# Linear attention inside a four-layer kernel: two batches' exponents moved to the head's begin, one score moved ahead of a product, and ten loops written out

## The reference, cut to what matters

```python
# attention B, batch size 4, 256 tokens, 16 heads, key size 128, value size 256
q = silu(causal_group_conv(h @ Wq.T));  k = silu(causal_group_conv(h @ Wk.T))   # 4 taps, one group per head
v = h @ Wv.T
gate = sigmoid(h @ Wg.T + bg);  beta = sigmoid(h @ Wb.T + bb)
def step(St, xs):                       # over the 256 tokens
    St = bt[..., None, None] * St + kt[..., None] * vt[:, :, None, :]
    ot = einsum('bhk,bhkv->bhv', qt, St) * gt[..., None]
out = outs @ Wo.T
```

## Time and profile before

| | |
|---|---|
| median of the runs | 1483.29 us |
| profiled execution | 1482.8 us, span 1481.0 us |
| TensorE busy | 1420.5 us, 96% of the span |
| VectorE, ScalarE, GpSimd busy | 61%, 58%, 55% |
| granted TensorE clock, mean | 0.992 of full |
| attention B, heads | about 752 to 1214 us of the span |
| feed-forward layers | about 452 to 704 us and 1214 to 1481 us |

### The profile page before, as it was taken

The page is one execution under the profiler, slowest core; times in us unless marked ns, Lnnn a source line. Parts: engine busy times, 40 slices in busy tenths (PEclk is TensorE's granted clock), DMA queues, the critical chain, the costliest instruction groups (busy, mean ns, idle before and its releaser), DMA issues. The chain is left out here.

```text
span 1481.0 us, 24095 instructions
## 1 busy us (share of the span) xinstructions
PE 1420.5 (96%) x8354; PEld 1228.3 (83%) x8360; DVE 901.3 (61%) x1719; ACT 861.7 (58%) x1737; POOL 819.8 (55%) x685
## 2 busy tenths in 40 slices
PE   7799999999999999999999999999999989999998
PEld 5589888898876778887689999999999976778886
DVE  6776766767665434334777777777777764443434
ACT  5566656666654433333587777777777755343332
POOL 4744444444433555554367767776777624455553
PEclk9999999999999999999999999999999999999999
DMA  2122232322311111110222212221222011111111
GB/s 82 32 69 72 70 70 69 71 67 71 73 31 50 43 53 43 43 52 21 79 69 71 64 54 60 71 64 54 61 70 64 19 39 33 43 42 53 42 53 39
DMA packets 48603, 82.48 MB, mean 56 GB/s; under 512 B 4256, under 2 KB 29984, under 8 KB 48288
## 3 DMA queue, kind: packets, MB, share of 16 engines
q1 hardware_dynamic: 48544, 81.70, 20.5%
HBM read 80.38 MB, written 1.31 MB: 55 GB/s over the span
## 5 line engine op out<-in xcount | busy, mean ns | idle before, releaser
L424 POOL TENSOR_TENSOR ms_a_lo<-m_a,ms_a_hi 128x384 fp32r<-128x384 f32 x128 | 129.9, 1015 | 200.4 <-ACT ms_a_hi L420 200.4
L1112 DVE TENSOR_TENSOR f_h<-f_sc,ps 128x512 f32<-128x512 f32 x112 | 76.4, 682 | 182.6 <-POOL f_sc L1044 182.6
L243 PE MATMUL ps<-xn_hi,fgu_hi 128*128 128x512 f32 x448 | 177.1, 395 | 5.1 <-DVE f_h L1112 4.8
L245 PE MATMUL ps<-xn_hi,fgu_lo 128*128 128x512 f32 x448 | 178.4, 398 | 0.0
L244 PE MATMUL ps<-xn_lo,fgu_hi 128*128 128x512 f32 x448 | 177.0, 395 | 0.0
L1114 DVE TENSOR_TENSOR fh_lo<-f_h,fh_hi 128x512 fp32r<-128x512 f32 x112 | 107.2, 957 | 98.3 <-ACT fh_hi L420 98.3
L993 ACT ACTIVATE f_s<-ps 128x512 f32<-128x512 f32 x112 | 66.7, 597 | 161.2 <-PE ps L245 161.0
L1044 POOL TENSOR_TENSOR f_sc<-f_s,coef_r 128x512 f32<-128x512 f32 x88 | 114.0, 1296 | 67.5 <-ACT f_s L993 67.5
L420 ACT CAST fh_hi<-f_h 128x512 fp32r<-128x512 f32 x112 | 69.1, 617 | 124.9 <-DVE f_h L1112 124.8
L424 POOL TENSOR_TENSOR fd_lo<-fw_raw,fd_hi 128x256 fp32r<-128x256 f32 x56 | 52.1, 930 | 125.8 <-ACT fd_hi L420 125.8
L243 PE MATMUL ps<-xn_hi,aw_hi 128*128 128x512 f32 x256 | 109.0, 426 | 7.4 <-DVE bmat_lo L727 7.4
(11 more groups left out here) (281 smaller groups left out, 4820.4 us busy)
## 6 DMA issues: line engine op xcount, KB each, us to landing
fw_raw<-ffn_w SPq DMA_DIRECT2D x56, 384.0 KB, 3.0
rows_a<-a_rows_d SPq DMA_DIRECT2D x64, 256.0 KB, 4.8
wconv_raw<-b_conv SPq DMA_DIRECT2D x16, 513.0 KB, 3.6
aw_raw<-a_heads SPq DMA_DIRECT2D x32, 256.0 KB, 5.2
wvo_raw<-b_vo SPq DMA_DIRECT2D x16, 512.0 KB, 3.5
rows_b<-b_rows_d SPq DMA_DIRECT2D x32, 256.0 KB, 4.9
wqk_raw<-b_qk SPq DMA_DIRECT2D x16, 256.0 KB, 4.8
x<-xT SPq DMA_DIRECT2D x2, 512.0 KB, 4.8
```

The lines of the kernel that those rows point to most:

```text
L243: nc.tensor.matmul(o, w[0], v[0], start=first, stop=False, skip_group_check=True)
L245: return nc.tensor.matmul(o, w[1], v[0], start=False, stop=last, skip_group_check=True)
L424: return nc.gpsimd.tensor_tensor(dst[1], src, f32(dst[0]), ALU.subtract).then_inc(sem(done_sem), 1)
L1112: nc.vector.tensor_tensor(f_h[:, c], f_sc[:, c], ps[:, 2 + c, :], ALU.mult).then_inc(sem("f_h"), 1)
```

## The change

In attention B, VectorE makes the exponents of batches 0 and 1 before it turns to the next head's fold and projections, and ScalarE makes their exponentials behind the two casts of k and ahead of the copies of the projections. ScalarE's casts of m_b keep their places among the casts of the values, but for batch 1, which loses the exponential in front. VectorE's exponents get a wait that the two batches of the head before are multiplied. TensorE computes score 2 ahead of value product 0. And all `Fori` loops of attention B and of the feed-forward layers become Python loops, so that their code is written out and the head is a constant.

```diff
@@ b_head_pe
             make("values")
+            b_score_pe(pe, h, p, 2, last)
             b_value_pe(pe, h, p, 0, last)
-            b_score_pe(pe, h, p, 2, last)
             b_score_pe(pe, h, p, 3, last)
@@ b_head_act
             if not last:
                 make("fold")
                 b_k_hi_act(act, h, p)
+                b_score_act(act, h, 0)
+                b_score_act(act, h, 1)
                 make("qk0", "qk1")
+            else:
+                b_score_act(act, h, 0)
+                b_score_act(act, h, 1)
             values = (lambda i: None) if last else (lambda i: b_values_act(act, h + 1, 1 - p, i))
             values(0)
-            b_score_act(act, h, 0)
+            b_split_act(act, h, 0)
             values(1)
-            b_split_act(act, h, 0)
-            b_score_act(act, h, 1)
+            b_split_act(act, h, 1)
             values(2)
-            b_split_act(act, h, 1)
             values(3)
@@ b_exponents_dve
-            if b >= 2:
+            if BATCH * h + b >= 2:
                 dve.wait_ge(sem("b_m_done"), BATCH * h + b - 1)
@@ b_head_dve
-            make("fold", "qk0", "qk1")
             for b in range(2):
                 b_exponents_dve(dve, h, b)
+            make("fold", "qk0", "qk1")
@@ f_pe, f_act, f_pool, f_dve, f_sp, b_pe, b_act, b_dve, b_pool, b_sp: each of the ten loops, as
-            with pe.Fori(0, B_HEADS // 2 - 1) as h2:
+            for h2 in range(0, B_HEADS // 2 - 1):
```

More of the change, by code:

```diff
@@ L919, in f_pe @@
             f_up_pe(pe, f, S_TILES, 0)
-            with pe.Fori(S_TILES // 2, F_TILES // 2 - 1) as i2:
+            for i2 in range(S_TILES // 2, F_TILES // 2 - 1):
                 for p in range(2):
@@ L970, in f_act @@
             f_up_weights_act(act, f, S_TILES + 1, 1)
-            with act.Fori(S_TILES // 2, F_TILES // 2 - 1) as i2:
+            for i2 in range(S_TILES // 2, F_TILES // 2 - 1):
                 for p in range(2):
@@ L1028, in f_pool @@
             pool.wait_ge(sem("f_coef_ready"), f_count(f, "coef_ready", 1))
-            with pool.Fori(S_TILES // 2, F_TILES // 2 - 1) as i2:
+            for i2 in range(S_TILES // 2, F_TILES // 2 - 1):
                 for p in range(2):
@@ L1072, in f_dve @@
                     f_route_dve(dve, f, step)
-            with dve.Fori(S_TILES // 2, F_TILES // 2) as i2:
+            for i2 in range(S_TILES // 2, F_TILES // 2):
                 for p in range(2):
@@ L1121, in f_sp @@
                 sp.dma_start(fw_raw[:, p], ffn_w[p * P:(p + 1) * P, :]).then_inc(sem(f"f_w_loaded{p}"), 16)
-            with sp.Fori(0, F_TILES // 2 - 1) as i2:
+            for i2 in range(0, F_TILES // 2 - 1):
                 for p in range(2):
@@ L1334, in b_act @@
             act.wait_ge(sem("b_ncum"), 1)
-            with act.Fori(0, B_HEADS // 2 - 1) as h2:
+            for h2 in range(0, B_HEADS // 2 - 1):
                 b_head_act(act, 2 * h2, 0, False, True)
@@ L1471, in b_dve @@
             b_make_dve(dve, 0, 0, ["conv1"])
-            with dve.Fori(0, B_HEADS // 2 - 1) as h2:
+            for h2 in range(0, B_HEADS // 2 - 1):
                 b_head_dve(dve, 2 * h2, 0, False)
@@ L1591, in b_pool @@
             b_conv_pool(pool, 0, 0, 1)
-            with pool.Fori(0, B_HEADS // 2 - 1) as h2:
+            for h2 in range(0, B_HEADS // 2 - 1):
                 b_head_pool(pool, 2 * h2, 0, True, True)
@@ L1661, in b_sp @@
                 sp.dma_start(rows_b[:, c], rows_of(b_rows_d, 0, c)).then_inc(sem(f"b_rows_loaded{c}"), 16)
-            with sp.Fori(0, B_HEADS - 2) as h:
+            for h in range(0, B_HEADS - 2):
                 for name, raw, src in B_PARTS:
```

## The result

The changed kernel takes 1490.25 us (median of 5 runs, 1489.03 to 1491.16), the kernel before 1483.29 (five runs by now, 1481.26 to 1484.62): the ratio is 1.0048, 95% interval 1.0033 to 1.0062, so 0.5% slower. The forecast was 1488.9.

What follows compares the result with a forecast made beforehand. TensorE, busy 96% of the span, was taken as the bound, so only its waits or added work matter. Terms -15.0 + 18.8 + 1.8 + 0 = +5.6 us gave 1488.9 us, range 1484.0 to 1494.0.

Steps and rivals of the forecast that it cites:

- The wait that goes: TensorE's wait at value product 0 for GpSimd's low part of the scores vanishes in heads 0 to 14: -15.0 us.
- The wait that comes: TensorE's k projection waits for ScalarE's q copy, delayed by four exponentials: 1.25 us in each of 15 heads, +18.8 us.
- The convolution's third block: TensorE reaches this block too early for VectorE's chain: 0.15 us late, 0.12 more than before, +1.8 us in all.
- The loops: Writing out the loops in attention and feed-forward stages changes nothing: 0, bounds -2 and +2 us.
- the fall of the clock: Rival: the new wait in each head lowers TensorE's clock, 25 us more, 1514 us; chance 0.05.
- The wash: Rival: stalls only change places, exponentials cost 1.1 us a head, convolution's wait does not grow: 1483 to 1486; chance 0.21.
- The faster rival: The q copy has slack, so the exponentials are hidden and only the old wait's removal counts: 1468 us; chance 0.08.

Runs made afterwards that it cites:

- e5: Changed kernel, exponentials of batches 0 and 1 in ScalarE's idle places inside the projections' casts, score 2 back behind value product 0: 1469.62 us, ratio 0.9915.
- e2: Kernel before, loops kept, with only score 2 moved ahead of value product 0: 1483.88 us, ratio 1.0005.
- e4: Changed kernel, exponentials of batches 0 and 1 moved into ScalarE's idle places inside the projections' casts: 1472.48 us, ratio 0.9936.
- e6: Changed kernel, only batch 0's exponentials ahead of the q copy, batch 1's back behind the first values cast: 1480.34 us, ratio 0.9979.
- e7: Changed kernel's order with its loops kept as loops, heads 0 and 1 written out in front: 1494.51 us, ratio 1.0076.
- e3: Changed kernel with score 2 put back behind value product 0: 1487.95 us, ratio 1.0031.
- e1: Kernel before with nothing but its ten loops written out: 1482.16 us, ratio 0.9992.
- e10: The kernel of e5 measured again, loops written out, beside e11 on one chip: 1467.33 us, ratio 0.9893.
- e11: The kernel of e9 measured again, loops kept, beside e10 on one chip: 1467.59 us, ratio 0.9892.
- e9: The order of e5 with loops kept as loops, heads 0 and 1 written out in front: 1467.20 us, ratio 0.9894.
- e8: Changed kernel with the order of e4 in head 0 alone, all other heads as in the changed kernel: 1489.24 us, ratio 1.0044.

## Why the prediction was right

The direction, the place and the sizes of the two large terms held. That the sum in the heads came out to a tenth is partly luck, since small errors of the terms cancel: per head the new wait costs 1.19 net (forecast 1.25), the convolution 0.20 (0.12), and the old wait gives back 1.09 (1.06), which makes 0.30 (0.31). Of the 7.1 us between the spans, by TensorE's landmarks: 0.6 lie ahead of attention B, in code that the change leaves alone (the first load lands 0.9 later); 3.4 in heads 0 and 1, up to head 1's score, of which 1.1 is the clock; 3.6 in the twelve periods up to head 13's, 0.30 each; 0.4 in the next; -0.7 in the last, where the old wait goes and no head is made; -0.2 in the feed-forward layer. Without the clock and the parts outside attention B this is +5.6, the forecast.

1. *The wait that goes.* Right in the whole: it is gone in heads 0 to 14, and e5 shows that with it out, and nothing in its place, the head loses 1.1 us, as counted. Wrong in an aside: "the score alone would have removed two thirds of it". It removes two thirds of the gap, and nothing of the time (e2), for the same chain of VectorE and ScalarE stops TensorE at the convolution. The slack that I had put at 1.2 us is about 1.9: GpSimd's first low part is ready near 918.7, value product 0 starts at 920.67. The text ahead of the prediction says that ScalarE's casts of m_b keep their places, but by the diff each goes one cast of the values earlier (in the trace, 917.11 behind the first and 918.17 behind the second, where they stood behind the second and third). No run takes this apart from the moved exponents, so its share in the gain of 1.1 is not known.
2. *The wait that comes.* Forecast 1.25 us per head; measured 1.12 + 0.11 = 1.23, less the 0.04 of before 1.19, in every head that makes a next one. e4 takes it away by moving two calls, e6 halves it, e7 keeps it without the written-out code: shown.
3. *The convolution's third block.* Forecast 0.12 more than before; measured 0.24 late plus 0.07 restart, 0.2 more than before, and 0.27 by e3. Right kind, half the size. The chain of VectorE took 7.44 us, between the 7.3 and 7.49 that I had worked out, and TensorE's own way 7.20 for 7.22; I had taken 0.15 out of a span of 0.1 to 0.27, counting on 0.15 from the faster answer of written-out code. Against e7 with its loops (7.54) it gave 0.10.
4. *The loops.* Forecast 0; e1 gives -1.0 us with an interval of -2.5 to +0.1, e10 against e11 nothing. In the changed kernel's order the loop form is slower (e7), by 0.1 us a head, at the convolution alone.

The term that was mis-sized is head 0. I had given the fall of the clock a chance of 0.05 as something that strikes all heads or none. It struck only the head where it was already there: the wait of 1.2 us came on top of one of 1.86, and the stretch at 1.2 GHz was longer, 1.1 us. That makes up most of the 1.4 us by which the forecast of +5.6 fell short of the 7.0 of the medians. The long stretch came in three of the four traces with this idle (the changed kernel, its repeat and e3, not e7), so the 1.1 us was no certain part of the change either. My reading that the trace before has one fall of the clock, at the longest idle of the stage, was wrong too: head 15 waits 2.43 us, up to 1199.40, and has a low stretch of its own (0.50 over 1200 to 1203). The Trainium skill, "TensorE: Matmul & The Clock Gate", section HAM oscillation, ties the penalty to idles that are long enough; by that rule, as in the trace, the 0.95 us of the other heads passed at full speed. Length alone does not settle it in these traces, though: 1.86 us lowered the clock in eight kernels of nine, and 2.31 us elsewhere did not.

The wash (0.21) needed the inserted exponentials to cost 1.1 and the convolution nothing; it missed by about 0.1 and 0.2 a head. The bounds of the parts, simply added, give -0.5 to +14.8, not +1.5 to +13; the range holds the result either way. The faster rival needed slack at the q copy; there was none.

## What to carry to other kernels

Before moving work off a wait's chain, look at the engine that is to take it earlier: what stands right behind the new place, and does anyone wait for it to the tenth of a microsecond? A handover without any idle on either side (904.84 to 904.98) is not slack but a wait of zero length, and it does not show in a list of waits. The free places are the idle gaps of the moved engine itself: the same four instructions that cost 18 us in front of the copy cost nothing 2.7 and 6.4 us later, in ScalarE's own waits. And when one chain of an engine ends two waits of another, filling the first only feeds the second; shorten the chain.

## What the runs showed of the hardware

The length of an idle did not settle by itself whether and how long the granted clock fell. At the k projection of head 0, nine kernels idle 1.86 us: eight then have 3.4 us at the lower level, and e10 none:

```profile
755.54 0.50 PE L243 MATMUL ps<-xn_hi,wqk_hi 128*128 128x512 f32 x1 [1.86 <-ACT q L1353]
...
755.50:759.50 4.00, 3.96 (x22) 1.00 0.15 55
```

After 2.45 us (e6) it was 3.4 us, after 3.05 three times 6.8 and once 3.4. The kernel before idles 1.94 us at 720.26 and 2.31 at 1269.17 and keeps the full clock at both. Idles of 1.04 and of 0.95, in fourteen heads, never lowered it.

In the written-out kernels e1, e3, e5 and e10, but not in the looped e9 and e11, one head (the eighth) is 0.3 us longer. In each of the four it is the convolution's third block that comes 0.3 late, and ahead of it VectorE's copy of the first block (L1507 or L1510), which starts 0.3 to 0.4 us later behind the multiplication than in the other heads (1.06 instead of 0.67 us in e5). Where that block waits in every head (the changed kernel, e4, e6, e8), 0.03 to 0.05 of it is left. Instruction loads rise from 36 packets and 0.59 MB in the kernel before to those of this line of the page after (queue, packets, MB, share):

```profile
q8 instruction: 67, 1.10, 0.3%
```

That they cause the 0.3 us was not tried.
